# An audio tower in one program: the attention projection tile by tile, the next group's WKV products ahead of the current projection, all rounds ordered anew, and expert results added straight to the output

## The reference, cut to what matters

```python
h = tok(x)                       # softmax over each pair of neighbours, weighted sum
h = h + rwkv(ln(h))              # k, v, r products; WKV recurrence along the 128 tokens; product with Wo
h = h + mlp(ln(h))               # 192 -> 768, exact gelu, 768 -> 192
a = ln(h)                        # layer 1
h = h + a + attention(a)         # 12 heads of 16, q and k normed over 192; softmax over the queries
h = h + experts(ln(h))           # 8 experts, best 2 of each token; 192 -> 768 -> 192 each
```

## Time and profile before

| | |
|---|---|
| three runs | 2091.97, 2093.18 (median), 2100.26 us |
| profiled execution: own time, span | 2086.18 us, 2084.4 us |
| busy share of the span: TensorE, VectorE, ScalarE, POOL | 85%, 71%, 59%, 35% |
| mean granted TensorE clock | 0.874 of full |
| tower phase, expert phase, last copy | to 1484 us, 1484 to 2063 us, 2063 to 2084 us |

### The profile page before, as it was taken

The page is one execution under the profiler, slowest core; times in us unless marked ns, Lnnn a source line. Parts: engine busy times, 40 slices in busy tenths (PEclk is TensorE's granted clock), DMA queues, the critical chain, the costliest instruction groups (busy, mean ns, idle before and its releaser), DMA issues.

```text
span 2084.4 us, 32990 instructions
## 1 busy us (share of the span) xinstructions
PE 1776.7 (85%) x10605; PEld 1384.4 (66%) x10605; DVE 1471.4 (71%) x2705; ACT 1230.0 (59%) x3205; POOL 737.6 (35%) x756
## 2 busy tenths in 40 slices
PE   2478989889889889899898897874799999999992
PEld 1345666657657567566666675553699999999992
DVE  3566686776876866866868758232698998999981
ACT  1236766765775676667657656552666666666660
POOL 0001122221321231231222213222377777767772
PEclk9789889889789899798898797765899999999996
DMA  3000000010010010010000100043676767667655
GB/s 80 12 4 16 23 22 29 24 37 23 28 36 23 28 36 23 24 34 28 21 25 26 36 8 29 22 149 103 176 177 150 181 154 171 165 161 177 148 118 141
DMA packets 119429, 149.49 MB, mean 72 GB/s; under 512 B 16948, under 2 KB 100007, under 8 KB 119271
## 3 DMA queue, kind: packets, MB, share of 16 engines
q1 hardware_dynamic: 86944, 114.23, 18.1%
q0 software_dynamic: 28608, 32.66, 8.9%
q10 hardware_dynamic: 3814, 1.83, 0.4%
HBM read 100.14 MB, written 54.83 MB: 74 GB/s over the span
## 4 chain that ended last, share of the span: by engine, by line
PE 69%; DVE 14%; ACT 6%; issue 5%; DMA 2%; POOL 2%; SPq 0%; ACTq 0%; POOLq 0%; DVEq 0%
PE ps L762 11%; PE ps L535 8%; PE ps L775 8%; PE ps L543 6%; PE ps L466 6%; PE ps L627 5%; PE ps L458 4%; PE ps L777 4%; PE ps L611 3%; DVE nmax L1356 3%; PE ps L475 3%; PE ps L559 3%; PE ps L638 2%; ACT probs L900 2%; DVE q_s L1287 2%
## 5 line engine op out<-in xcount | busy, mean ns | idle before, releaser
L1158 POOL DMA_INDIRECT total<-ey,etoken x156 | 275.6, 1767 | 156.7 <-DMA total<-ey,etoken 65.3
L900 ACT ACTIVATE probs<-ps,nmax 128x128 f32<-128x128 f32 x768 | 271.6, 387 | 49.3 <-DVE nmax L1356 49.2
L775 PE MATMUL ps<-w_hl,h_hi 128*128 128x384 f32 x936 | 274.6, 364 | 3.8 <-DVE ey L1578 3.8
L1035 ACT ACTIVATE h_full<-ps,eb 128x512 f32<-128x512 f32 x234 | 167.7, 717 | 162.8 <-PE ps L762 162.7
L777 PE MATMUL ps<-w_hl,h_lo 128*128 128x192 f32 x936 | 235.6, 252 | 0.0
L627 PE MATMUL ps<-probs,vpad 128*32 128x128 f32 x1536 | 105.6, 377 | 100.0 <-DVE vpad L1366 94.7
L777 PEld LDWEIGHTS ps<-w_hl,h_lo 128*128 128x128 f32 x936 | 180.5, 193 | 0.0
L775 PEld LDWEIGHTS ps<-w_hl,h_hi 128*128 128x128 f32 x936 | 177.4, 190 | 4.5 <-issue 4.4
L535 PE MATMUL ps<-hTB,w_up 96*128 96x512 f32 x384 | 175.4, 609 | 2.5 <-ACT hTB L877 2.2
L900 ACT ACTIVATION_READ_ACCUMULATOR probs<-ps,nmax 128x1 f32 x768 | 174.1, 227 | 0.0
L1148 POOL TENSOR_TENSOR w_lo<-w_raw,w_hi 128x1536 fp32r<-128x1536 f32 x39 | 157.6, 4042 | 36.3 <-ACT w_hi L1016 36.3
(11 more groups left out here) (227 smaller groups left out, 3945.4 us busy)
## 6 DMA issues: line engine op xcount, KB each, us to landing
w_raw<-in_L_ffn_w SPq DMA_DIRECT2D x39, 576.0 KB, 4.7
ex<-expert_rows_in SPq DMA_DIRECT2D x39, 528.0 KB, 5.1
w_raw<-in_L_ffn_w SPq DMA_DIRECT2D x39, 384.0 KB, 5.4
w_raw<-in_L_ffn_w SPq DMA_DIRECT2D x78, 192.0 KB, 5.7
xt<-in_x SPq DMA_DIRECT2D x16, 768.0 KB, 4.5
expert_rows_in<-xt SPq DMA_DIRECT2D x17, 528.0 KB, 7.4
total<-resC SPq DMA_DIRECT2D x16, 384.0 KB, 2.6
eb<-in_L_ffn_b SPq DMA_DIRECT2D x39, 96.0 KB, 3.6
```

The lines of the kernel that those rows point to most:

```text
L775: nc.tensor.matmul(ps[:, 4 + s, 0:2 * C], h_hi[b][:, m, q], w2_hl[b][:, m, :], start=(m == 0), stop=False)
L900: last = nc.scalar.activation(probs[:, t % 2, HJ * c + j, :], ps[:, 4 + j, c * P:(c + 1) * P], ACT.Exp, bias=nmax[:, t, j, c:c + 1], accum ...
L1035: nc.scalar.activation(h_full[:, m, :], ps[:, m % 4, :], ACT.Gelu, bias=eb1[u][:, m:m + 1])
L1158: nc.gpsimd.indirect_dma_start(total, bass.IndirectOffsetOnAxis(ap=etoken[u][:, s:s + 1], axis=0), ey[b][:, s, :], None, compute_op=ALU.ad ...
```

## The change

1. **Projection in bank 3.** `c_project(g, t)` writes each tile to bank 3, columns 0 to 191, and signals each tile. `c_attn_add(g, t)` adds one tile (128x192) and takes its statistics one tile later; tile t + 1 of the projection waits for the addition of tile t. `a_project` no longer waits for `hF_ready`, `b_transposes` and SyncE's store now count it in tiles.
2. **Products of the next group first.** `a_hidden`, `a_r` and `a_k` of group gn run inside the round of ga's projection and before its `a_v` (which opens the next round). Since hA of the next group is then written before ga's residual reads its own, SyncE copies hA to a new tensor `hA_kept` (384 KB in SBUF), and `a_residual` reads that.
3. **Rounds ordered anew** on all four engines.
4. **Experts add to the output.** `total` is now `out` itself; the indirect additions skip padding rows by a bound (`bounds_check`); the spare rows, their one DMA and the last copy are gone.

Diff of the functions:

```diff
-    total = nc.dram_tensor("total", (NB * T + ET, C), F32).ap()
+    total = out.rearrange("b p c -> (b p) c")
...
             def store_h(g):
-                sp.wait_ge(S["hF_ready"], g + 1)
+                sp.wait_ge(S["hF_ready"], G * (g + 1))
...
+            def keep_h(g):
+                sp.wait_ge(S["a_stats"], g + 1)
+                if not isinstance(g, int) or g > 0:
+                    sp.wait_ge(S["hB_ready"], g)
+                sp.dma_start(hA_kept[:, :, :], hA[:, :, :]).then_inc(S["h_kept"], 16)
...
             with sp.Fori(2, NG - 1) as i:
                 load_x(i + 1)
+                keep_h(i)
                 store_h(i - 2)
...
-            sp.dma_start(out.rearrange("b p c -> (b p) c"), total[0:NB * T, :]).then_inc(S["out_stored"], 16)
-            sp.wait_ge(S["out_stored"], 16)
...
             def a_delta(g):
-                    pe.wait_ge(S["hB_ready"], g)
+                    pe.wait_ge(S["v_ready"], g)
             def a_hidden(g):
+                    pe.wait_ge(S["hB_ready"], g)
-            def a_project(g, gc):
+            def a_project(g, ga):
-                    pe.wait_ge(S["hF_ready"], gc + 1)
+                    pe.wait_ge(S["tanh_ready"], ga + 1)
             def b_transposes(g):
+                    pe.wait_ge(S["hF_ready"], G * (g - 1))
-            def c_project(g, t, ga):
+            def c_project(g, t):
                 pe.wait_ge(S["oT_ready"], G * g + t + 1)
+                if t == 0:
+                    pe.wait_ge(S["qT_ready"], G * g + G)
+                else:
+                    pe.wait_ge(S["hF_ready"], G * g + t)
...
+                    last = nc.tensor.matmul(ps[:, 3, 0:C], oT[0:rows, t % 2, c, :], w_ao[0:rows, c, :],
...
+                        ey[b][:, s, :], None, bounds_check=NB * T - 1, oob_is_err=False,
...
             def a_tokens(g):
+                    dve.wait_ge(S["h_kept"], 16 * g)
             def a_residual(g):
+                dve.wait_ge(S["h_kept"], 16 * (g + 1))
...
-            def c_attn_add(g):
+            def c_attn_add(g, t):
+                dve.wait_ge(S["aproj_psum"], G * g + t + 1)
+                if t == 0:
+                    dve.wait_ge(S["res_ready"], g + 1)
+                nc.vector.tensor_tensor(resC[:, t, :], ps[:, 3, 0:C], resC[:, t, :],
+                                        ALU.add).then_inc(S["hF_ready"], 1)
+                if t > 0:
+                    dve.wait_ge(S["hF_ready"], G * g + t)
+                    nc.vector.bn_stats(statsR[:, t - 1, :], resC[:, t - 1, :])
...
```

More of the change, by code:

```diff
@@ L690, in round_ @@
                 if gc is not None: c_scores(gc, 2, 0)
+                if gn is not None: a_r(gn)
                 if gc is not None: c_scores(gc, 2, 1)
                 if gc is not None: c_queries(gc, 3, gb)
+                if gn is not None: a_k(gn)
                 if gc is not None: c_values(gc, 1, gb)
                 if gc is not None: c_scores(gc, 3, 0)
-                if gc is not None: c_project(gc, 0, ga)
+                if gc is not None: c_project(gc, 0)
                 if gc is not None: c_scores(gc, 3, 1)
[L697 to L717, removed]
             pe.wait_ge(S["weights_in"], 16 * N_LOADS)
@@ new lines, in round_ @@
+                if gb is not None: transposed(gb, "b", hTB, 2)
+                if gr is not None: r_out(gr)
+                if gc is not None: c_qkv(gc, 3)
+                if gb is not None: b_gelu(gb, 0)
+                if gr is not None: transposed(gr, "r", hTC, 4)
+                if gb is not None: b_gelu(gb, 1)
+                if gb is not None: b_gelu(gb, 2)
+                if gc is not None: c_k_norm(gc)
+                if gb is not None: b_gelu(gb, 3)
+                if gn is not None: a_delta(gn)
@@ L964, in round_ @@
[L964 to L968, removed]
-                if gn is not None: a_gate(gn)
             loads = [
@@ L1373, in c_values @@
                     vch.end()
-            def c_attn_add(g):
-                dve.wait_ge(S["aproj_psum"], g + 1)
-                dve.wait_ge(S["res_ready"], g + 1)
-                r2 = resC[:, :, :].rearrange("p (h t) c -> p h (t c)", h=2)
-                nc.vector.tensor_tensor(r2, ps[:, 0:2, 0:2 * C], r2, ALU.add).then_inc(S["hF_ready"], 1)
-                dve.wait_ge(S["hF_ready"], g + 1)
-                ln_stats(g, "r", resC, statsR, mvR)
+            def c_attn_add(g, t):
+                chain = lns["r"]
+                dve.wait_ge(S["aproj_psum"], G * g + t + 1)
[6 more added lines that the diff above has]
+                    nc.vector.bn_stats(statsR[:, t - 1, :], resC[:, t - 1, :])
+                if t == G - 1:
+                    dve.wait_ge(S["hF_ready"], G * g + G)
+                    chain.begin(g)
+                    chain.link(nc.vector.bn_stats(statsR[:, t, :], resC[:, t, :]), stand_alone)
+                    for n in range(G):
+                        last = nc.vector.bn_aggr(mvR[:, n, :], statsR[:, n, :])
+                    last.then_inc(S["r_stats"], 1)
+                    chain.end()
             def pad_fill():
@@ L1445, in round_ @@
             def round_(i):
-                gn, ga, gb, gc, gr, _ = stages(i)
-                if gr is not None: c_values(gr, 2)
+                _, ga, gb, gc, gr, gs = stages(i)
+                if gb is not None: a_scan_q(gb)
+                if gb is not None: a_denominator(gb)
+                if ga is not None: a_delta(ga)
+                if gr is not None: c_qk_stats(gr)
+                if gb is not None: a_reciprocal(gb, 0)
                 if gb is not None: a_reciprocal(gb, 1)
-                if gr is not None: c_max(gr, 3, 1)
+                if gs is not None: r_pick(gs)
@@ L1481, in round_ @@
-                if ga is not None: a_denominator(ga)
-                if ga is not None: a_reciprocal(ga, 0)
-                if gc is not None: c_max(gc, 3, 0)
+                if gs is not None: r_place(gs)
+                if gb is not None: a_numerator(gb)
+                if gr is not None: c_keys(gr, 0)
+                if gr is not None: c_keys(gr, 1)
+                if gr is not None: c_keys(gr, 2)
+                if gr is not None: c_keys(gr, 3)
+                if ga is not None: a_tokens(ga)
@@ new lines, in round_ @@
+                if gb is not None: a_gate(gb)
+                if gr is not None: c_max(gr, 0, 0)
+                if gr is not None: c_max(gr, 0, 1)
+                if gc is not None: b_mlp_add(gc, gr)
+                if gb is not None: a_residual(gb)
+                if gr is not None: c_max(gr, 1, 0)
+                if gr is not None: c_max(gr, 1, 1)
+                if gr is not None: c_values(gr, 0)
+                if ga is not None: a_mix(ga)
+                if gr is not None: c_max(gr, 2, 0)
@@ new lines, in round_ @@
+                if gr is not None: c_max(gr, 2, 1)
+                if gb is not None: b_stats(gb)
+                if gr is not None: c_values(gr, 1)
+                if gr is not None: c_max(gr, 3, 0)
+                if gr is not None: c_values(gr, 2)
+                if gr is not None: c_max(gr, 3, 1)
+                if gr is not None: c_attn_add(gr, 0)
+                if ga is not None: a_exponents(ga)
+                if gr is not None: c_attn_add(gr, 1)
+                if ga is not None: a_fraction_args(ga)
```

186 lines of the change are left out of this document (88 added, 98 removed).

## The result

The changed kernel takes **2126.88 us** (median of four runs, 2124.54 to 2132.12) against 2094.55 before: ratio 1.0154, interval 1.0125 to 1.0183. It is slower by 32 us; 1948 was forecast. The profiled execution has a span of 2122.7 us and a mean clock of 0.865.

What follows compares the result with a forecast made beforehand. TensorE, busy 85% of the span, was taken to lose tower time to pauses and low clock. 174 + 14 x 72 + 178.7 = 1360.7; + 578.6 + 1.8 = 1941, or 1948 us on the runs' scale; range 1875 to 2035.

Steps and rivals of the forecast that it cites:

- So 67.6 us at full clock: Result of walking one new tower round through the engines' ordered lists: 67.6 us if the clock stays full.
- I take 3: Low clock in the attention stretch once a round, slowing `a_r`, score halves and values: 2 to 4 us, taken as 3.
- P = 72: Forecast length of one steady tower round: 72 us, own bounds 68 and 76.
- 1360.7: Forecast start of the first full expert product: 174 + 14 x 72 + 178.7 us.
- First term: TensorE's work in one tower round at full clock, summed from its pieces in the old trace: 60.5 us.
- rival 2: Low clock through the whole attention stretch, 19.5 us of matmuls becoming 39: P = 78, 2032 us; chance 0.22.
- Second term: Low clock in a new round, expected once, in the attention stretch: 3 us.
- The walk: Step-by-step count of one new round from the third attention addition, lists taken in order, 0.1 us a handoff: 67.6 us.
- the wait for x: VectorE waits 2.6 us for the x load in `a_delta`; with no slack behind it, said to count fully.
- The rule of the Trainium skill: Short pauses between matmul groups move the clock repeatedly; by it the attention stretch would be low throughout, 2032 us.
- rival 4: Slower: the bound makes each of the 156 indirect adds dearer; at 1.3 us more, 2134 us; chance 0.06.
- the bound at 0: Expert phase: bounding the indirect adds was taken to cost 0, with 0.6 us an add as upper bound.

Runs made afterwards that it cites:

- x_early: The changed kernel with SyncE's store one iteration later, so that x is there when VectorE wants it; 2087.0 us, 0.998 of the kernel before.
- exps_first_x: r_later with ScalarE's first-half exponentials ahead of the next group's ln_out, and x_early's later store; 1967.9 us, 0.939 of the kernel before.
- r_later: The changed kernel, reordered: ScalarE's qkv 3 and gelu 0 before r_out, gelu 1 before transposed r; TensorE's MLP-up 2 before r_transposes; 2012.7 us, 0.960 of before.

## Why the prediction was wrong

- **Which step failed.** "So 67.6 us at full clock", the low clock at "I take 3", and with them P = 72. The rounds measured 85.3. The first full expert product came 181.5 us later than the forecast's 1360.7 (1542.2). Of these, 166 lie in the fourteen rounds from group 1's MLP-up to group 15's (184.06 to 1358.05, 83.9 each; the first and the last are shorter than 85.3), 10 in the fill (184 for 174) and 5 in the drain (184.2 for 178.7). In a steady round the 13.3 us too few are 5.5 of work, 10.1 of low clock, and 2.3 of pauses and handoffs the other way.
- **First term: the work, 60.5, is 66.0.** The earlier trace rows shows 0.94 us for *twelve* score matmuls, which are one half of a tile; the sum took 0.45 for a half. That is 3.4 us of the 5.5 by itself (8 x (0.87 - 0.45), with 0.87 from start to start); the rest is spread over the other pieces. The same slip put the old low clock at 12.6 when it was 8.1, and so promised more to win than there was; it is also in the 19.5 us of work in the attention stretch, by which rival 2 was priced.
- **Second term: the low clock, 3, is 13.1.** The stretch in the attention came where it was forecast (`a_r` from 3.6 to 7.0), but costs 6.4 us. The second stretch, in the MLP-up, was not foreseen at all. It costs (7.54 - 5.2) + (3.78 - 1.8) + (1.91 - 0.9) + (3.42 - 1.7) = 7 us (6.6 by the clock's records).
- **Where it came from.** The walk has no term for POOL's rstd r. It took 1.9 us before (643.21 to 645.14); it takes 5.0 because the new order of VectorE puts scan_q and denominator beside it, and `r_out` ended 8.2 us after the last addition (599.2 - 591.0). The list was read for its waits, not for what two engines hold in common.
- **The pauses were right in sum** (6.2; some 7 in the walk, and 1.4 for handoffs), and the wait for x was there: 1.4 us in the round shown, longest 2.3, for 2.6 forecast. That it "counts fully" was not so: without it `x_early` gained 2.7 us a round, more than the wait, and by the clock, not by shorter pauses.
- **The rule of the Trainium skill** (short pauses while banks change hands move the clock, "TensorE: Matmul & The Clock Gate", "A second HAM failure mode: psum-queue depth-cycling") was closer than the sum. It was priced for the attention stretch alone; the granted clock shows the fall behind short pauses (2.28 and 0.92 us) in the MLP-up as well.
- **The rivals.** Rival 2 (P = 78) named the clock, but not the place: 13.7 us of the attention stretch were low, not all of it, and half of the cost lay in the MLP-up; rival 4, the slower case, named the bounded adds, which cost nothing. The slower case that happened, the low clock also falling where TensorE's work is densest, was not among them. With 6 in 100 for slower the chances were far too sure.
- **Right:** the copy, 21.0 measured for 21.1; the bound at 0; `hA_kept` (5.6 us from issue to landing, above its upper bound of 4.5) hidden; POOL's scatter hidden; `vpad` gone as the releaser of long pauses in the steady rounds (0.8 us at most, 3.9 before). That `exps_first_x` comes to P = 72.8 does not bear out the forecast of 72: it is another order, and its split, 66.6 + 2.6 + 4.0, is not the forecast's 60.5 of work either.

## What to carry to other kernels

When TensorE is near the bound, price a new order by the clock at which each stretch will run, not by pauses alone: a pause of 2 us ahead of dense work cost 7 us here, and matmuls thrown away in it were repaid. An engine's small operations on the path of another (here rstd on POOL) belong beside VectorE work with an input in PSUM or with a single input (`shiftC` took 0.24 us beside `hB`; `shiftB`, in the kernel before, 0.23 beside the statistics of qk), not beside two-input work in SBUF. Where a short step waits for a slow side chain, let what does not need it go first in the list: such swaps, two on ScalarE and one on TensorE, turned +1.5% into -5.5%.

## What the runs showed of the hardware that was not expected

- Operations of POOL on 128x4 numbers last as long as the two-input VectorE operation beside them: 2.29 against 2.29 us, 1.25 against 1.22, and 1.05 against 0.96.
- A TensorE that was fully busy from 602 us on stayed at 1.2 GHz to 615 us; four dense MLP-up matmuls at the start of that stretch did not bring the clock back, and transposes and logits followed them.
- In `r_later` the rounds repeat in threes (72.6, 78.3, 77.8 us) with `a_r` at 3.67, 6.4 and 7.1 us: the same program, the same order, another clock from round to round.
- The bound on an indirect add costs nothing measurable (1767 and 1786 ns without it, 1748 to 1801 with it), and the adds go to the output as fast as to a scratch tensor.
